# One slope behind the loop and a share of the scaled one-hot copies on GpSimd, in the logit stage of a graph network kernel

## The chip, the cores and the metric

The kernel runs on one core of a Trainium2 chip. The metric is the device time of one execution in microseconds; the median of several runs is quoted, and one execution is profiled. Engines are called as the profile calls them: PE (TensorE), DVE (VectorE), ACT (ScalarE), POOL (GpSimd), SP (SyncE, which only issues DMAs here).

## The reference

Four graph layers run one after the other over 3125 nodes and 100000 edges sorted by destination; each is followed by a layer norm over `x + layer(x)`. The change lies in the second layer, an attention layer. What is computed there:

```
h  = x @ Wn.T + bn;   e = edge_attr @ We.T + be
a  = leaky_relu(sum((h[src] + e) * attn, -1), 0.01)      # one logit per edge
m  = segment_max(a, dst)                                 # largest logit of each destination
a  = exp(a - m[dst]);  a = a / segment_sum(a, dst)[dst]
out = relu(segment_sum(h[src] * a, dst))
```

The leaky ReLU with slope 0.01 is max(z, 0.01 z), and it rises with z, so the largest logit of a node is the leaky ReLU of its largest z.

## The kernel before

Nodes are cut into 25 blocks of 125; edges are sorted into chunks of 128 (one edge for each partition), and a "group" is ten chunks. Each edge has one-hot rows, stored in DRAM as bf16, that say which node of a block it points to. The stage in question is `phase_logits` (tiles whose names begin with `lm_` in the trace). It computes z for each edge, the logit, and `negated`, which holds minus the largest logit of each destination node. The logits are kept in the second word of `words` (`srt_words` in the trace; a column of every second float, 4992 columns) and go on to the attention phase that follows.

The main loop runs over 119 groups, in 25 blocks of destination nodes. For each group g:

- SP loads the group's source plane (`load_planes`, line 1163) and its two halves of one-hot rows (`load_hot`, line 1171) into rings of four buffers. Before it refills a ring slot it waits for the engine that read it: `expanded` for the planes, `lifted` for the one-hot rows.
- DVE expands the plane into a one-hot of source nodes (`expand`, line 1217); PE looks the node values up in ten small products (`look`, line 1356), in three bf16 parts.
- DVE adds the three parts (line 1223, `total`), adds the edge part kept in `logit` (line 1225), applies the slope (line 1229) and subtracts a floor, a lower bound of all logits, so that what is stored is not negative (line 1230, `logits`). This raises `ready`.
- ACT multiplies each of the ten chunks' one-hot rows with the edge's value (line 1322) into one of two `raised` buffers and raises `lifted`. It waits for `ready`, for the one-hot rows, and for `grouped`, which says that DVE has read the buffer two groups back.
- DVE merges the raised buffer into `top8`: a copy for the first group of a block (line 1237), a maximum for the others (line 1239, `greater`). At the end of a block it reduces `top8` over the ten chunks (line 1288).

The order on DVE is written out by hand in `step(g)`: `expand(g + 3)`, then total and logits of group g + 2, then `greater(g)`. So PE has from the end of one `expand` to the `total` of the next step for its look, and ACT works one to two groups ahead of `greater`. Behind the loop PE transposes the 25 blocks of maxima (line 1371), DVE takes the maximum over the partitions (line 1300), builds diagonal matrices (line 1303), and PE spreads these over all partitions (line 1376). GpSimd does a single memset in this stage (line 1328).

A `Chain` object raises a semaphore with an instruction and makes its engine wait for it, so that the next instruction may read the result.

Of the kernel before, what the change touches and what calls it, by code (L numbers as in the profile page):

```python
# [8 lines left out]
ALU = mybir.AluOpType  # L9
ACT = mybir.ActivationFunctionType  # L10
AX = mybir.AxisListType
ds = bass.ds
# [5 lines left out]
P = 125  # L18
NB = N // P
EC = E // P  # L20
L = 128
# [3 lines left out]
RING = 4  # L25
# [142 lines left out]
def turns_of(eng, k):  # L168

    return eng.value_load(k["group_start"][0:1, 30:31], min_val=1, max_val=NT)  # L170
# [961 lines left out]
def phase_logits(nc, k, logit, negated, scratch):  # L1132
    ctx = ExitStack()
    with ctx:
# [14 lines left out]
        hot_landed, hot_arrived = [s.sem(f"hot_landed{r}") for r in range(RING)], s.sem("hot_arrived")  # L1149
        arrived, flipped, copied, written = (s.sem(n) for n in ("arrived", "flipped", "copied", "written"))  # L1150
        bounded, gathered, floored, cleared = (s.sem(n) for n in ("bounded", "gathered", "floored", "cleared"))
        split, chain_sem = s.sem("split"), s.sem("chain")
        expanded, looked, summed, ready, lifted, grouped = (
            s.sem(n) for n in ("expanded", "looked", "summed", "ready", "lifted", "grouped"))
        joined, passed, turned, ended = (s.sem(n) for n in ("joined", "passed", "turned", "ended"))
        PZ = 4

        with nc.Block() as block:

            @block.sync  # L1160
            def _(sp):
                def load_planes(g, j):
                    sp.dma_start(planes[:, j % RING, :], k["src_rows"][ds(G * g, G), :].rearrange("c l -> (c l)").partition_broadcast(L)
                                 ).then_inc(landed[j % RING], 16)

                unit_at = Offsets(sp, s, "unit", k["unit_at"], NUA - 1)

                def load_hot(g, j):
                    unit_at.load(g)
                    for t, unit in enumerate(unit_at.pair()):  # L1170
                        sp.dma_start(hot[:, j % RING, HALF * S * t:HALF * S * t + HALF * S],
                                     k["hot"][DST][ds(unit, 1), :, :].rearrange("o p n -> (o p) n")).then_inc(hot_landed[j % RING], 16)

                for b in range(BLOCKS):
                    if b % BANKS == BANKS - 1 or b == BLOCKS - 1:
                        b0 = b // BANKS * BANKS
                        sp.wait_ge(copied, b + 1)
                        sp.dma_start(k["src_rows"][b0 * L:(b + 1) * L, :].rearrange("(b c) l -> c b l", c=L), rows[:, b0:b + 1, :]
                                     ).then_inc(written, 16)
                load_hot(0, 0)  # L1180
                sp.wait_ge(written, 16 * WRITES)
                for j in range(3):
                    load_planes(j, j)
                sp.wait_ge(landed[0], 16)
                sp.sem_inc(arrived, 1)
                def turn(i, last):
                    for j in range(RING):
                        g = RING * i + j
                        sp.wait_ge(expanded, g + 2)
                        sp.sem_inc(passed, 1)  # L1190
                        load_planes(g + 3, j + 3)
                        sp.wait_ge(landed[(j + 1) % RING], 16 * (i + (j + 1) // RING) + 16)
                        sp.sem_inc(arrived, 1)
                        sp.wait_ge(lifted, g + 1)
                        sp.sem_inc(passed, 1)
                        if not last or j < 3:
                            load_hot(g + 1, j + 1)
                        sp.wait_ge(hot_landed[j], 32 * i + 32)
                        sp.sem_inc(hot_arrived, 1)

                turns = full_turns_of(sp, k)
                with sp.Fori(0, turns) as i:
                    turn(i, False)
                turns = full_turns_of(sp, k)
                turn(turns, True)
                for j in range(1, 3):
                    sp.wait_ge(landed[j], 16 * turns + 32)
                    sp.sem_inc(arrived, 1)

            @block.vector  # L1210
            def _(dve):
# [9 lines left out]
                def total(chain, g):  # L1221
                    dve.wait_ge(looked, g + 3)
                    chain(v.tensor_reduce(z[:, :], ps[:, ds((g % PZ) * 512, 3 * G)].rearrange("p (c t) -> p c t", t=3), AX.X, ALU.add))
                    dve.sem_inc(summed, 1)  # L1224
                    chain(v.tensor_tensor(z[:, :], z[:, :], logit[:, ds(G * g, G)], ALU.add))

                def logits(chain, g):
                    at = logit[:, ds(G * g, G)]
                    chain(v.scalar_tensor_tensor(z[:, :], z[:, :], 0.01, z[:, :], ALU.mult, ALU.max))
                    v.tensor_scalar(at, z[:, :], floor[:, :], None, ALU.subtract).then_inc(ready, 1)  # L1230

                def greater(g, first):
                    lift = raised[:, ds(g % 2, 1), :].rearrange("p a n -> p (a n)")
                    dve.wait_ge(lifted, g + 4)
                    dve.wait_ge(grouped, g + 2)
                    if first:
                        ins = v.tensor_copy(top8[:, :], lift)  # L1237
                    else:
                        ins = v.tensor_tensor(top8[:, :], top8[:, :], lift, ALU.max)
                    ins.then_inc(grouped, 1)  # L1240
# [10 lines left out]
                v.tensor_copy(v3[:, :, 2], rest[:, :]).then_inc(split, 1)  # L1251
                dve.wait_ge(gathered, 1)
                chain(v.tensor_reduce(low[:, 0:2], bank(7)[0:1, 0:2 * L].rearrange("p (t l) -> p t l", t=2), AX.X, ALU.min))
                chain(v.tensor_tensor(low[:, 2:3], low[:, 0:1], low[:, 1:2], ALU.add))
                v.scalar_tensor_tensor(low[:, 3:4], low[:, 2:3], 0.01, low[:, 2:3], ALU.mult, ALU.max).then_inc(bounded, 1)
                dve.wait_ge(gathered, 2)
                chain(v.tensor_copy(floor[:, :], bank(7)[:, 256:257]))
                for sem, head in ((summed, PZ), (grouped, 2), (joined, 1), (expanded, 2)):
# [2 lines left out]
                expand(1)  # L1261
                total(chain, 0)
                expand(2)
                logits(chain, 0)
                dve.wait_ge(ready, 1)
                total(chain, 1)
                logits(chain, 1)
                n = chain.n
                dve.sem_inc(passed, 1)

                def step(g, first):
                    chain = Chain(dve, chain_sem, n + 3 * g)
                    expand(g + 3)
                    dve.wait_ge(ready, g + 2)
                    total(chain, g + 2)
                    logits(chain, g + 2)
                    greater(g, first)
                    assert chain.n == 3

                with dve.Fori(0, NB) as d:  # L1280
                    g0, g1 = group_range(dve, k, d)
# [9 lines left out]
                with dve.Fori(g1, turns_of(dve, k) * RING) as g:  # L1291
                    dve.wait_ge(looked, g + 4)
                    dve.sem_inc(expanded, 1)
                    dve.wait_ge(looked, g + 5)
                    dve.sem_inc(summed, 1)
                    dve.sem_inc(ready, 1)
                    dve.wait_ge(lifted, g + 4)
                    dve.sem_inc(grouped, 1)
                dve.wait_ge(turned, 1)
                v.tensor_reduce(greatest[:, :], ps[0:P, 0:NB * L].rearrange("p (b l) -> p b l", l=L), AX.X, ALU.max).then_inc(ended, 1)  # L1300
                dve.wait_ge(ended, 1)
                for b in range(NB):
                    ins = v.tensor_scalar(diag[:, b, :], k["ident"][0:P, 0:P], greatest[:, b:b + 1], -1.0, ALU.mult, ALU.mult)
                ins.then_inc(ended, 1)
# [4 lines left out]
            @block.scalar  # L1309
            def _(act):  # L1310
                for b in range(BLOCKS):
                    act.wait_ge(flipped, b + 1)
                    nc.scalar.copy(rows[:, b, :], bank(b % BANKS)[:, 0:L]).then_inc(copied, 1)
                act.sem_inc(lifted, 3)
                with act.Fori(0, turns_of(act, k)) as i:
                    for j in range(RING):
                        g = RING * i + j
                        act.wait_ge(ready, g + 1)
                        act.wait_ge(hot_arrived, g + 1)
                        act.wait_ge(grouped, g + 1)  # L1320
                        for c in range(G):
                            ins = nc.scalar.activation(raised[:, j % 2, c * P:(c + 1) * P], hot[:, j, c * S:c * S + P], ACT.Copy,  # L1322
                                                       scale=logit[:, ds(G * g + c, 1)])
                        ins.then_inc(lifted, 1)

            @block.gpsimd
            def _(pool):
                nc.gpsimd.memset(ones[:, :], 1.0).then_inc(cleared, 1)

            @block.tensor  # L1330
            def _(pe):
# [8 lines left out]
                ins.then_inc(gathered, 1)  # L1340
                pe.wait_ge(cleared, 1)
                pe.wait_ge(bounded, 2)
                t_.matmul(bank(7)[:, 256:257], ones[0:1, :], low[:, 3:4], start=True, stop=True).then_inc(gathered, 1)
                pe.wait_ge(split, 1)
                pe.wait_ge(copied, BLOCKS)
                at = Offsets(pe, s, "at", k["block_at"], HALF * (HALF - 1))
# [1482 lines left out]
```

## Time and profile before

| what | value |
|---|---|
| median of 3 runs | 4012.24 us (3999.35 to 4015.62) |
| the profiled execution | 4001.7 us, of which the span is 4000.0 us |
| main loop of the logit stage | 1990 to 2416 us of the span, 426 us |
| its tail, to the copy of `negated` | 2416 to 2445 us |
| DVE, ACT, PE and POOL busy in the loop | 358.7, 356.2, 168.4 and 0 us |

Times in the profile are microseconds from the start of the span, single durations nanoseconds where marked. A row of the timeline gives start, length, engine, line, operation, output and inputs, the count of instructions merged into it, and in brackets how long the engine sat idle before it and what released it. A row of the groups gives the busy time of all instructions of one line, the mean length of one, and the idle time before them with its releasers. ACT's instructions overlap in part, so forty of 385 ns fill 11.84 us.

### The profile page before, as it was taken

How to read it: one execution, taken by the hardware profiler on the slowest of the kernel's cores; microseconds unless marked ns; L12 is line 12 of the kernel's file. 1: busy time of each engine (PE TensorE's matmuls, PEld its weight loads, DVE VectorE, ACT ScalarE, POOL GpSimd, SP SyncE). 2: the span in 40 equal slices, each digit the busy share in tenths (PEclk: the TensorE clock that was granted, in tenths of full speed). 3: DMA queues.
4: the chain of work that ended last, by engine and by line, in shares of the span. 5: the costliest groups of instructions: out<-in, count | busy, mean ns of one | idle time of the engine just before them, and what ended most of it. 6: DMA issues, size and time to landing. Idle time of an engine off the chain costs nothing. (4 is left out here: it accounts for less than half of the span.)

```text
span 4000.0 us, 83948 instructions
## 1 busy us (share of the span) xinstructions
PE 3158.0 (79%) x17737; PEld 2344.7 (59%) x17738; DVE 2479.1 (62%) x6639; ACT 1821.9 (46%) x6302; POOL 1235.7 (31%) x993
## 2 busy tenths in 40 slices
PE   5666667988887777989743335889999899999978
PEld 4444445888876756767632224778888444444455
DVE  7999998978875563234488886777766500001754
ACT  1888883344445542011298875777776000000111
POOL 1688888888888800111000000000000000002512
PEclk9999999999998888999855557999999999999989
DMA  2444445677878874767565553544332543541067
GB/s 96 125 121 121 123 121 116 183 215 237 239 239 273 274 275 143 230 194 207 163 213 184 183 168 108 151 130 119 113 98 79 188 138 109 192 154 55 0 219 254
DMA packets 438541, 654.87 MB, mean 164 GB/s; under 512 B 102707, under 2 KB 293812, under 8 KB 438314
## 3 DMA queue, kind: packets, MB, share of 16 engines
q1 hardware_dynamic: 350648, 516.48, 41.7%
q10 hardware_dynamic: 56434, 125.33, 8.7%
q0 software_dynamic: 31360, 11.85, 3.3%
q8 instruction: 49, 0.80, 0.1%
q14 instruction: 50, 0.41, 0.0%
HBM read 436.96 MB, written 215.57 MB: 163 GB/s over the span
## 5 line engine op out<-in xcount | busy, mean ns | idle before, releaser
L1069 POOL DMA_INDIRECT slots<-all_B,put_index x800 | 1044.9, 1306 | 343.2 <-issue 341.1
L2338 PE MATMUL gio_po<-gio_T,all_A 125*128 125x500 f32 (+1 forms) x1400 | 529.8, 540 | 6.1 <-DMA gio_T<-pair 6.1
L2338 PEld LDWEIGHTS gio_po<-gio_T,all_A 125*128 125x128 f32 x1400 | 249.4, 190 | 283.2 <-issue 276.4
L1322 ACT ACTIVATE lm_raised<-lm_hot,srt_words 128x125 f32<-128x125 bf16 x1200 | 356.2, 385 | 81.0 <-DVE lm_top L1237 63.8
L1356 PE MATMUL lm_ps<-lm_v,lm_node 125*128 x1220 | 170.5, 184 | 264.4 <-DVEq L1224 94.5
L1040 PE MATMUL put_ps<-put_right_in,put_left_in 128*128 128x125 f32 x2210 | 320.0, 295 | 66.3 <-ACT put_left_in L897 65.8
L2085 PE MATMUL att_ps<-att_right,att_left 128*125 128x125 f32 x2380 | 313.5, 285 | 70.5 <-ACT att_right L2106 67.3
L1635 PE MATMUL c_po<-c_halves,c_T 125*125 125x512 f32 x1250 | 330.0, 413 | 22.8 <-DMA c_T<-counts 13.1
L2085 PEld LDWEIGHTS att_ps<-att_right,att_left 128*125 128x125 f32 x2380 | 283.9, 189 | 96.1 <-issue 85.8
L1040 PEld LDWEIGHTS put_ps<-put_right_in,put_left_in 128*128 128x128 f32 x2210 | 282.1, 203 | 90.3 <-ACT put_left_in L897 76.2
L2159 DVE SCALAR_TENSOR_TENSOR att_power<-soft_negated,srt_words,att_far 128x125 f32 (+1 forms) x1190 | 320.4, 345 | 3.7 <-ACT att_right L2106 3.3
L1356 PEld LDWEIGHTS lm_ps<-lm_v,lm_node 125*128 125x128 bf16 x1220 | 127.0, 104 | 307.9 <-issue 283.8
L1044 PE MATMUL put_ps<-put_right_out,put_left_out 128*128 128x125 f32 x2210 | 303.8, 287 | 0.0
L2647 DVE SCALAR_TENSOR_TENSOR upd_pre<-sum_u,sum_sums,upd_bias 125x512 f32<-125x512 f32 x25 | 27.7, 1109 | 423.6 <-POOL upd_bias L2561 422.8
L1635 PEld LDWEIGHTS c_po<-c_halves,c_T 125*125 125x125 f32 x1250 | 232.5, 190 | 95.6 <-DVE c_halves L1727 21.7
L897 ACT CAST put_left_in<-put_hot 128x640 f32 (+1 forms) x221 | 161.5, 731 | 275.8 <-DVE put_hot L811 159.9
L1044 PEld LDWEIGHTS put_ps<-put_right_out,put_left_out 128*128 128x128 f32 x2210 | 284.1, 204 | 0.8
L2057 PE MATMUL att_ps<-all_A,all_B 125*125 125x257 f32 x1250 | 277.5, 381 | 0.6 <-ACT att_sums L2110 0.6
L816 DVE TENSOR_TENSOR put_right_in<-put_hot,put_words_in 128x625 f32<-128x625 bf16 x224 | 181.9, 812 | 150.2 <-PE put_ps L1040 144.9
L2106 ACT ACTIVATE att_right<-att_power 128x250 f32<-128x250 f32 x595 | 242.9, 408 | 55.2 <-DVE att_power L2159 54.0
L2103 ACT CAST att_left<-att_ring 128x250 f32 x595 | 229.2, 385 | 74.8 <-SPq L231 39.1
L2057 PEld LDWEIGHTS att_ps<-all_A,all_B 125*125 125x125 f32 x1250 | 231.5, 187 | 38.9 <-issue 0.9
(440 smaller groups left out, 5308.0 us busy)
## 6 DMA issues: line engine op xcount, KB each, us to landing
c_T<-counts SPq DMA_DIRECT2D x255, 312.5 KB, 3.4
pair<-put_T ACTq DMA_DIRECT2D x125, 625.0 KB
att_ring<-hot SPq DMA_DIRECT2D x480, 160.0 KB
gio_T<-pair SPq DMA_DIRECT2D x60, 1250.0 KB, 5.9
hot<-put_hot SPq DMA_DIRECT2D x448, 160.0 KB
all_A<-in_edge_attr_dram SPq DMA_DIRECT2D x100, 448.0 KB
lm_planes<-src_rows SPq DMA_DIRECT2D x123, 320.0 KB, 3.6
counts<-put_T ACTq DMA_DIRECT2D x125, 312.5 KB
```

What stands on the lines that cost most here:

```text
L1040: ins = t_.matmul(tile(1, c), left_in[:, c, :], right_in[:, c, :], start=False, stop=False, skip_group_check=True)
L1044: ins = t_.matmul(tile(2, c), left_out[:, c, :], right_out[:, c, :], start=False, stop=False, skip_group_check=True)
L1069: nc.gpsimd.indirect_dma_start(slots, bass.IndirectOffsetOnAxis(index[:, C * g + j:C * g + j + 1], 0), stage[:, C * g + j, :], None).then_ ...
L1322: ins = nc.scalar.activation(raised[:, j % 2, c * P:(c + 1) * P], hot[:, j, c * S:c * S + P], ACT.Copy, scale=logit[:, ds(G * g + c, 1)])
L1356: ins = t_.matmul(bank(j % PZ)[0:L, 3 * c:3 * c + 3], node[0:P, j % 2, L * c:L * c + L], v3[:, ds(units[c // HALF], HALF), :][:, c % HALF, :],
L1635: return t_.matmul(po[0:P, d % BANKS, 0:2 * width], T[0:P, n % LOOK, t * P:(t + 1) * P].bitcast(fp32r), halves[:, PB * q + t, :], start=(q ...
L2057: ins = t_.matmul(product(0), T[h][:, q, :], H[:, q, 0:width], start=(q == 0), stop=(q == NB - 1))
L2085: ins = t_.matmul(tiles_of(ps)[:, ds(units[(W * f + c) // HALF], HALF), :][:, (W * f + c) % HALF, 0:P], left[:, f, c, :], right[:, f, c, : ...
L2103: nc.scalar.copy(left[:, f, :, :], ring.slot(r, lf, W * f, W * f + W)).then_inc(left_ready.sem(f), 1)
L2106: nc.scalar.activation(right[:, f, :, :], power[:, f, :, :], ACT.Exp).then_inc(right_ready.sem(f), 1)
L2159: ins = v.scalar_tensor_tensor(power[:, f, c, :], negated[:, ds(d, 1), :].rearrange("p a n -> p (a n)"), logit[:, ds(G * g + q, 1)], far[: ...
L2338: ins = t_.matmul(po[:, i % 2, h, 0:w], A[:, b, 128 * h:128 * h + 128], tiles, start=(b == 0), stop=(b == NB - 1))
```

## The change

1. `total` no longer ends with the sum of node part and edge part, and `logits` is gone. One instruction, `(z - floor) + at`, writes the value without the slope and raises `ready`; two of DVE's small operations of each group go. The floor is made without the slope too (one operation less ahead of the loop).
2. Behind the loop a new `slope` adds the floor back and applies the slope, in two instructions over all 4992 columns of `logit`; after the maxima over the partitions it does the same for the 125 by 25 maxima. It stands ahead of DVE's wait for PE's transposes and waits for ACT's last group.
3. ACT makes eight of a group's ten scaled copies. GpSimd makes the other two in one `tensor_tensor` product over 2 x 125 elements: the one-hot rows (bf16) times the two values (f32, each spread over 125 elements), into the same `raised` buffer (f32). It waits for the same three semaphores as ACT and raises `hoisted`. SP's refill of the one-hot ring and DVE's `greater` wait for `hoisted` beside `lifted`.

```diff
-                    chain(v.tensor_tensor(z[:, :], z[:, :], logit[:, ds(G * g, G)], ALU.add))
-
-                def logits(chain, g):
                     at = logit[:, ds(G * g, G)]
-                    chain(v.scalar_tensor_tensor(z[:, :], z[:, :], 0.01, z[:, :], ALU.mult, ALU.max))
-                    v.tensor_scalar(at, z[:, :], floor[:, :], None, ALU.subtract).then_inc(ready, 1)
+                    v.scalar_tensor_tensor(at, z[:, :], floor[:, :], at, ALU.subtract, ALU.add).then_inc(ready, 1)
+
+                def slope(t, parts):
+                    chain(v.tensor_scalar(t, t, floor[0:parts, :], None, ALU.add))
+                    chain(v.scalar_tensor_tensor(t, t, 0.01, t, ALU.mult, ALU.max))
...
                     dve.wait_ge(lifted, g + 4)
+                    dve.wait_ge(hoisted, g + 4)
...
+                turns = turns_of(dve, k)
+                dve.wait_ge(lifted, turns * RING + 3)
+                chain = Chain(dve, sloped)
+                slope(logit, L)
                 dve.wait_ge(turned, 1)
                 v.tensor_reduce(greatest[:, :], ...).then_inc(ended, 1)
                 dve.wait_ge(ended, 1)
+                slope(greatest[:, :], P)
...
-                        for c in range(G):
+                        for c in range(LIFTS):
...
+                pool.sem_inc(hoisted, 3)
+                with pool.Fori(0, turns_of(pool, k)) as i:
+                    for j in range(RING):
+                        g = RING * i + j
+                        pool.wait_ge(ready, g + 1)
+                        pool.wait_ge(hot_arrived, g + 1)
+                        pool.wait_ge(grouped, g + 1)
+                        by_chunk = (lambda t, w: t.rearrange("p (c n) -> p c n", n=w)[:, :, 0:P])
+                        nc.gpsimd.tensor_tensor(by_chunk(raised[:, j % 2, LIFTS * P:], P), by_chunk(hot[:, j, LIFTS * S:], S),
+                                                logit[:, ds(G * g + LIFTS, G - LIFTS)].unsqueeze(2).to_broadcast([L, G - LIFTS, P]), ALU.mult
+                                                ).then_inc(hoisted, 1)
```

## Rows read from the trace of the kernel before

**Rows 1.** Busy times of the loop: PE, PEld, DVE, ACT, POOL, clock, DMA.

```profile
1990.00:2416.00 426.00, 168.37 (x1205) 125.39 (x1205) 358.68 (x746) 356.23 (x1200) 0.00 (x0) 0.50 0.59 183
```

**Rows 2.** Groups of instructions in the loop: busy us, mean ns, idle before.

```profile
L1322 ACT ACTIVATE lm_raised<-lm_hot,srt_words 128x125 f32<-128x125 bf16 x1200 | 356.2, 385 | 81.0 <-DVE lm_top L1237 63.8 <-DVE srt_words L1230 12.2 <-DVE lm_top L1239 3.6
L1239 DVE TENSOR_TENSOR lm_top<-lm_top,lm_raised 128x1250 f32<-128x1250 f32 x94 | 137.4, 1461 | 0.4
L1217 DVE TENSOR_SCALAR lm_node<-lm_planes,all_iop x119 | 65.3, 549 | 18.1 <-DVE soft_negated L1288 14.6 <-PE lm_ps L1356 2.1 <-SPq L1193 0.7
L1288 DVE TENSOR_REDUCE soft_negated<-lm_top 128x1250 f32 x25 | 62.2, 2486 | 3.7
L1225 DVE TENSOR_TENSOR lm_z<-lm_z,srt_words 128x10 f32<-128x10 f32 x120 | 20.4, 170 | 32.9 <-DVE lm_z L1223 32.8
L1237 DVE COPY lm_top<-lm_raised 128x1250 f32 x25 | 20.3, 812 | 0.1
```

**Rows 3.** Timeline of one block of five groups.

```profile
2103.63 0.55 DVE L1217 TENSOR_SCALAR lm_node<-lm_planes,all_iop  x1 [0.64 <-DVE soft_negated L1288]
...
2105.93 0.55 DVE L1217 TENSOR_SCALAR lm_node<-lm_planes,all_iop  x1
...
2106.66 0.19 DVE L1223 TENSOR_REDUCE lm_z<-lm_ps 128x10 f32 x1 [0.18 <-PE lm_ps L1356]
...
2109.15 0.55 DVE L1217 TENSOR_SCALAR lm_node<-lm_planes,all_iop  x1
2109.46 11.84 ACT L1322 ACTIVATE lm_raised<-lm_hot,srt_words 128x125 f32<-128x125 bf16 x40 [0.21 <-DVE lm_top L1239]
...
2112.09 0.55 DVE L1217 TENSOR_SCALAR lm_node<-lm_planes,all_iop  x1
2112.55 0.18 DVE L1223 TENSOR_REDUCE lm_z<-lm_ps 128x10 f32 x1
...
2113.01 0.17 DVE L1225 TENSOR_TENSOR lm_z<-lm_z,srt_words 128x10 f32<-128x10 f32 x1 [0.27 <-DVE lm_z L1223]
...
2113.43 0.23 DVE L1230 TENSOR_SCALAR srt_words<-lm_z,lm_floor 128x10 f32 x1
2113.66 1.46 DVE L1239 TENSOR_TENSOR lm_top<-lm_top,lm_raised 128x1250 f32<-128x1250 f32 x1
...
2115.04 0.55 DVE L1217 TENSOR_SCALAR lm_node<-lm_planes,all_iop  x1
...
2118.22 2.48 DVE L1288 TENSOR_REDUCE soft_negated<-lm_top 128x1250 f32 x1
...
2121.34 0.55 DVE L1217 TENSOR_SCALAR lm_node<-lm_planes,all_iop  x1 [0.64 <-DVE soft_negated L1288]
```

**Rows 4.** Timeline of SP's queue: plane loads of two turns, first block.

```profile
2013.48 0.33 SPq L1163 DMA_DIRECT2D lm_planes<-src_rows  x1
...
2015.96 0.33 SPq L1163 DMA_DIRECT2D lm_planes<-src_rows  x1
```

**Rows 5.** Timeline of other phases where GpSimd computes beside DVE.

```profile
3115.95 0.72 POOL L2253 TENSOR_TENSOR all_total<-all_total,all_X 125x256 f32<-125x256 f32 x1 [10.93 <-DVEq L2245]
...
3683.72 0.74 DVE L2647 SCALAR_TENSOR_TENSOR upd_pre<-sum_u,sum_sums,upd_bias 125x512 f32<-125x512 f32 x1
...
3689.28 1.66 POOL L2559 TENSOR_SCALAR upd_part<-sum_u,sum_sums 125x512 f32<-125x512 f32 x1 [0.79 <-DVE upd_pre L2650]
...
3691.02 1.36 POOL L2561 TENSOR_TENSOR upd_bias<-upd_part,sum_base 125x512 f32<-125x512 f32 x1
...
3691.75 1.18 DVE L2647 SCALAR_TENSOR_TENSOR upd_pre<-sum_u,sum_sums,upd_bias 125x512 f32<-125x512 f32 x1
```

**Rows 6.** Timeline behind the loop, and the reduction over the logit column.

```profile
2418.43 5.70 PE L1371 MATMUL lm_ps<-all_ident,soft_negated 128*125 128x128 f32 x25 [3.64 <-DVE soft_negated L1288]
2424.17 3.49 DVE L1300 TENSOR_REDUCE lm_greatest<-lm_ps 125x25 f32<-125x3200 f32 x1 [5.79 <-PE lm_ps L1371]
...
1970.90 5.35 DVE L1245 TENSOR_REDUCE lm_least<-srt_words 128x1 f32<-128x4992 f32 x1
```

More of the change, by code:

```diff
@@ L1151, in phase_logits @@
         bounded, gathered, floored, cleared = (s.sem(n) for n in ("bounded", "gathered", "floored", "cleared"))
-        split, chain_sem = s.sem("split"), s.sem("chain")
-        expanded, looked, summed, ready, lifted, grouped = (
-            s.sem(n) for n in ("expanded", "looked", "summed", "ready", "lifted", "grouped"))
+        split, chain_sem, sloped = s.sem("split"), s.sem("chain"), s.sem("sloped")
+        expanded, looked, summed, ready, lifted, hoisted, grouped = (
+            s.sem(n) for n in ("expanded", "looked", "summed", "ready", "lifted", "hoisted", "grouped"))
+        LIFTS = 8
         joined, passed, turned, ended = (s.sem(n) for n in ("joined", "passed", "turned", "ended"))
@@ L1194, in turn @@
                         sp.wait_ge(lifted, g + 1)
+                        sp.wait_ge(hoisted, g + 1)
                         sp.sem_inc(passed, 1)
@@ L1253, in _ @@
                 chain(v.tensor_reduce(low[:, 0:2], bank(7)[0:1, 0:2 * L].rearrange("p (t l) -> p t l", t=2), AX.X, ALU.min))
-                chain(v.tensor_tensor(low[:, 2:3], low[:, 0:1], low[:, 1:2], ALU.add))
-                v.scalar_tensor_tensor(low[:, 3:4], low[:, 2:3], 0.01, low[:, 2:3], ALU.mult, ALU.max).then_inc(bounded, 1)
+                v.tensor_tensor(low[:, 2:3], low[:, 0:1], low[:, 1:2], ALU.add).then_inc(bounded, 1)
                 dve.wait_ge(gathered, 2)
@@ L1263, in _ @@
                 expand(2)
-                logits(chain, 0)
                 dve.wait_ge(ready, 1)
                 total(chain, 1)
-                logits(chain, 1)
                 n = chain.n
@@ L1271, in step @@
                 def step(g, first):
-                    chain = Chain(dve, chain_sem, n + 3 * g)
+                    chain = Chain(dve, chain_sem, n + g)
                     expand(g + 3)
@@ L1275, in step @@
                     total(chain, g + 2)
-                    logits(chain, g + 2)
                     greater(g, first)
-                    assert chain.n == 3
+                    assert chain.n == 1
                 with dve.Fori(0, NB) as d:
@@ L1297, in _ @@
                     dve.wait_ge(lifted, g + 4)
+                    dve.wait_ge(hoisted, g + 4)
                     dve.sem_inc(grouped, 1)
+                turns = turns_of(dve, k)
+                dve.wait_ge(lifted, turns * RING + 3)
+                chain = Chain(dve, sloped)
+                slope(logit, L)
                 dve.wait_ge(turned, 1)
@@ L1342, in _ @@
                 pe.wait_ge(bounded, 2)
-                t_.matmul(bank(7)[:, 256:257], ones[0:1, :], low[:, 3:4], start=True, stop=True).then_inc(gathered, 1)
+                t_.matmul(bank(7)[:, 256:257], ones[0:1, :], low[:, 2:3], start=True, stop=True).then_inc(gathered, 1)
                 pe.wait_ge(split, 1)
```

## The prediction

> **What bounds the kernel now.** I read the loop's stretch first (busy times by engine), then its groups with their idle times, then the timeline of one block. In the loop, 426.0 us, DVE is busy 358.68 us and ACT 356.23 us; PE is busy 168.37 us, POOL not at all [rows 1]. Two engines with equal loads don't say which sets the pace; the idle columns do. ACT's 81.0 us of idle time are nearly all ended by DVE: 63.8 us by the copy L1237, the first merge of a block, 12.2 us by the first logits, 3.6 us by L1239 [rows 2]. DVE in turn waits for nobody who matters: before L1239 it sat idle 0.4 us in 94 merges and before L1237 0.1 us, so ACT is never late; PE and SP together end 2.8 us ahead of L1217. What DVE loses is its own: 32.8 us ahead of L1225 (the result of L1223 has to land first) and 14.6 us at the turn of a block [rows 2]. So DVE's order of work is the path. In the timeline the reader is to see the period of a step: the expansions start at 2109.15, 2112.09 and 2115.04, 2.945 us apart, and L1223, L1225, L1230 and L1239 follow with no gap but L1225's 0.27. The first step of a block has the shorter copy and takes 2105.93 - 2103.63 = 2.30 us; a whole block of five takes 14.59 us to the start of its reduction (2118.22) and 3.12 us from there to the next block (2121.34) [rows 3]. Copies (25), merges (94) and reductions (25) in [rows 2] give 119 steps in 25 blocks; the reductions of the timeline split them into one block of 18, two of 8, nine of 5, one of 4 and twelve of 3.
>
> **DVE's two operations.** From the start of L1225 to that of L1230 is 2113.43 - 2113.01 = 0.42 us; then L1230 takes 0.23 until L1239 starts at 2113.66 [rows 3]. The new instruction has the same column of floors as an operand as L1230, so I give it L1230's 0.23 us, and 0.42 us go from each step. The 0.27 us behind L1223 stay, since the new instruction reads z too. Its other results are awaited where they were: `ready` an expansion later, `lifted` and `hoisted` while the instruction runs. The second of the waits is taken to cost nothing because the sequencer does it under these 0.23 us; without that cover I would add some hundredths of a microsecond to each step. A step with a merge would become 2.945 - 0.42 = 2.53 us.
>
> **What PE gives back.** A look starts when its expansion is done and the next step's L1223 waits for it. The wait is visible once: L1223 at 2106.66 had waited 0.18 us for PE, 3.03 us after the expansion of 2103.63 [rows 3]. So L1223 can't come earlier than 3.03 us after the expansion of the step before. In the second step of each block this holds already; the 0.42 us that the first step gains are lost there again. The gain is thus 0.42 us for 119 - 25 = 94 steps, 39.5 us. Further on in a block the rule spans two steps: 3.03 us plus the 2.48 - 0.42 = 2.06 us from L1223 to the next expansion (2112.55 to 2115.04 before) is 5.09, or 2.55 us a step in place of 2.53. Over 69 steps that is 1.5 us. Left: 38 us.
>
> **ACT, SP and the memory.** Forty activations took 11.84 us [rows 3], 0.296 us each, so eight take 2.37 us a group in place of 2.96. That is under DVE's 2.53; ACT gains slack and the end gains nothing from it alone. Without it DVE's shorter step would have run into ACT's 2.96 us, so this part is what makes the first part worth anything. SP's plane loads follow each other 2.48 us apart where its queue doesn't wait [rows 4], with one more semaphore wait to come: below 2.55, but barely. Blocks of up to 8 are covered by the 3.12 us of the block turn; the first block, of 18 steps, starts without that lead and I charge 1 us. DMA's share of 0.59 [rows 1] would rise by a tenth, and the clock of TensorE, granted at 0.50 (the 1.2 GHz level) in this stretch [rows 1], is taken to stay.
>
> **GpSimd's product.** Nothing in the loop shows one. The nearest row is L2253, 256 f32 elements in 0.72 us; L2561 takes 1.36 us for 512 [rows 5], so 250 elements are about 0.7 us. It starts when `grouped` rises, some 0.2 us behind the end E of a merge (ACT had 0.21 us of idle time there [rows 3]), and is needed two steps later: as work it is hidden. What it can cost is DVE's time. [Rows 5] show it: L2647 takes 0.74 us where no POOL operation starts beside it and 1.18 us when it starts inside L2561, at 3691.75; it was held for 0.44 us, to 3692.19, 0.19 us ahead of L2561's recorded end (3692.38). In the new loop the instruction at risk is the new sum, which like L2647 reads two tiles of SBUF. It would start 0.92 us behind an expansion (2113.01 - 2112.09), which is E + 0.84 since the expansion starts 0.08 us before E (2115.04 against 2113.66 + 1.46). The product runs from E + 0.2 to E + 0.92 and lets go at E + 0.73: no delay. That is the low end; a gain below nothing is excluded, since the product takes over no DVE work. If it is itself held by the expansion, to E + 0.47, it lets go at E + 1.00, a delay of 0.16 us; if it then also holds to its recorded end, E + 1.19, the delay is 0.35 us. No row shows whether an expansion holds a product. I take 0.10 us, because part of a product's start can pass while it waits. It applies in the steps whose sum follows a merge within the same block by less than 1.5 us: all but the first two of a block (there the second waits for PE anyway, and behind the last merge the reduction lies), 119 - 50 = 69. Cost 7 us.
>
> The Trainium skill, SBUF — State Buffer, section Who interferes with whom, goes further: a DVE instruction with two SBUF inputs and a GpSimd one that reads SBUF exclude each other for the whole instruction, and a two-port DVE operation locks GpSimd out as well. The rows agree that DVE is held, and disagree by 0.19 us on how long. By that rule the delay is the 0.35 us above; it is the first rival below.
>
> **The tail.** Behind the last reduction DVE waited for PE's transposes, from 2418.43 to 2424.17 [rows 6]. The slope now fills this wait: two operations over 4992 columns. The reduction over the same column took 5.35 us [rows 6]; the second, with two inputs, gets this. The first has one input: 5.35 us at worst, at best the rate of the copy L1237 (1250 in 0.812 us [rows 2]), some 2.8 us for 4992, by an estimate that keeps its 0.16 us of overhead. Together 8.2 to 10.7 us, of which 5.7 lie beside the transposes: 2.5 to 5.0 us late. The slope of the maxima adds two instructions of about 0.2 us, on the path. I take 4.2 us. The floor's shorter chain ahead of the loop saves one small operation, 0.2 us, which I leave out: the first expansion waits for loads.
>
> **Sum.** 39.5 - 1.5 - 1 - 7 - 4.2 = 25.8 us saved, rounded to 26. Against the profiled execution (4001.7 us, span 4000.0) that is 3976 us. That execution lies 10.5 us under the median of the runs, which the forecast is for: 4012.24 - 26 = 3986 us. With the bounds (delay 0 to 0.25, tail 2.9 to 5.4) the saving is 14 to 34 us: 3978 to 3998.
>
> **Rivals.**
> - *The product holds the sum to its end* (0.35 us or a little more, up to 0.45). 69 steps cost 24 to 31 us, and of 37 us 2 to 9 are left behind the tail: about 4006 us, no change. For it: the 0.44 us of L2647. Against it: L2647 went on before the product ended. Chance 0.2.
> - *The product is long, and slower is the result.* Its input is bf16 and one operand is spread, and no row shows either on POOL. L2559 took 1.66 us [rows 5]. A product of that length, let go 0.19 us before its end and held by the expansion as above, ends at E + 0.47 + 1.66 - 0.19 = E + 1.94: 1.1 us of delay in 69 steps is 76 us against 37, so 43 us slower with the tail, 4055 us; at half that excess, 1.2 us of length, it is even. The point is a delay of (37 - 4.2) / 69 = 0.48 us. For it: unknown types. Against it: L2253 and L2561. Chance 0.12.
> - *SP sets the step.* If its turn is 2.75 us with the extra wait, long blocks gain half: 16 steps of the first and 12 of the blocks of 8, 0.2 us each, some 6 us. With the tail, 25 us of gain become 20: near the border. Chance 0.08, shared between faster and same.
>
> **How the numbers follow.** The forecast has 0.6. About 0.5%, 20 us, is what a measurement of this kernel tells from no change; the runs before spread over 16 us. The forecast's own range reaches below that bound at its far end, so of its 0.6 I put 0.51 to faster, 0.08 to same, 0.01 to slower; with SP's 0.04 and the rivals this makes faster 0.55, same 0.32, slower 0.13. The range runs from 3970, the best bound less the spread of the median, to 4014, which takes in the first rival and leaves out the long product.
>
> **What would show it.** Right: expansions 2.55 to 2.7 us apart within long blocks; one instruction of 0.23 us in place of L1225, L1229 and L1230; L1223 of second steps waiting some 0.6 us for PE; ACT idle between most groups; L1300 2.5 to 5 us later behind the last reduction than now. Wrong: a sum that takes 0.4 us or more beside a product, products over 1 us long, or expansions that wait for SP. A step under 2.5 us would say that PE's 3.03 us were read wrongly.

## The result and the profile after

The changed kernel takes 3979.3 us (median of 4 runs, 3976.4 to 3985.8), the kernel before 4007.7 us in 4 runs. The ratio is 0.9932, with a 95% interval of 0.9906 to 0.9958: 17 to 38 us less, by the medians 28 us. The forecast was 26 us less, 3986 us against 4012.2.

The profiled execution of the changed kernel has a span of 3984.1 us, 15.9 less than before; the stage itself explains more than that. From its first instruction on DVE to the end of the copy of `negated` it takes 449.1 us in place of 473.9, which is 24.8 us less; the other phases, in which nothing changed, happened to take 9 us longer in this execution. So the stage is compared here, not the span. Its parts:

| part of the stage | before | after | difference |
|---|---|---|---|
| up to the first step of the loop | 23.2 us | 23.1 us | -0.1 |
| loop: expansion of its first step to the end of the last reduction | 424.6 us | 395.3 us | -29.3 |
| tail: to the end of the copy of `negated` | 26.1 us | 30.7 us | +4.6 |

A block of five of the changed kernel in the timeline (the expansion is now L1219, the reduction of z L1225, the new sum L1228, copy and merge L1240 and L1242, GpSimd's product L1342):

```profile
2097.26 0.55 DVE L1219 TENSOR_SCALAR lm_node<-lm_planes,all_iop  x1 [0.64 <-DVE soft_negated L1287]
...
2099.22 0.55 DVE L1219 TENSOR_SCALAR lm_node<-lm_planes,all_iop  x1
...
2100.29 0.19 DVE L1225 TENSOR_REDUCE lm_z<-lm_ps 128x10 f32 x1 [0.53 <-PE lm_ps L1372]
...
2102.43 0.55 DVE L1219 TENSOR_SCALAR lm_node<-lm_planes,all_iop  x1
...
2102.80 0.63 POOL L1342 TENSOR_TENSOR lm_raised<-lm_hot,srt_words 128x250 f32<-128x250 bf16 x1 [2.58 <-DVE lm_top L1242]
...
2103.35 0.23 DVE L1228 SCALAR_TENSOR_TENSOR srt_words<-lm_z,lm_floor,srt_words 128x10 f32 x1 [0.28 <-DVE lm_z L1225]
2103.64 1.46 DVE L1242 TENSOR_TENSOR lm_top<-lm_top,lm_raised 128x1250 f32<-128x1250 f32 x1
...
2105.02 0.55 DVE L1219 TENSOR_SCALAR lm_node<-lm_planes,all_iop  x1
...
2107.61 0.55 DVE L1219 TENSOR_SCALAR lm_node<-lm_planes,all_iop  x1
...
2110.43 2.50 DVE L1287 TENSOR_REDUCE soft_negated<-lm_top 128x1250 f32 x1
```

Against [rows 3]: the first step takes 1.96 us in place of 2.30; the second still takes 3.21, and its reduction now waits 0.53 us for PE in place of 0.18; the steps after it take 2.59 in place of 2.945. The product runs for 0.63 us beside the expansion and the reduction and is over at 2103.43, 0.08 us behind the start of the sum, which takes its 0.23 us undisturbed. Behind the sum there is something new: the merge starts 0.29 us after the sum's start; before, it started 0.23 us after that of L1230.

The groups of the stage:

```profile
L1327 ACT ACTIVATE lm_raised<-lm_hot,srt_words 128x125 f32<-128x125 bf16 x960 | 291.0, 386 | 115.8 <-DVE lm_top L1240 70.7 <-DVE lm_top L1242 34.6 <-DVE srt_words L1228 10.5
...
L1242 DVE TENSOR_TENSOR lm_top<-lm_top,lm_raised 128x1250 f32<-128x1250 f32 x94 | 137.3, 1461 | 5.9
...
L1342 POOL TENSOR_TENSOR lm_raised<-lm_hot,srt_words 128x250 f32<-128x250 bf16 x120 | 75.4, 628 | 338.1 <-DVE lm_top L1242 199.1 <-DVE lm_top L1240 116.3 <-DVE srt_words L1228 18.9
...
L1228 DVE SCALAR_TENSOR_TENSOR srt_words<-lm_z,lm_floor,srt_words 128x10 f32 x119 | 27.3, 229 | 33.4 <-DVE lm_z L1225 33.4
L1225 DVE TENSOR_REDUCE lm_z<-lm_ps 128x10 f32 x119 | 21.8, 183 | 12.8 <-PE lm_ps L1372 12.8
```

ACT and POOL wait for DVE almost alone, as ACT did in [rows 2]; the merges now have 5.9 us of idle time ahead of them (0.4 before), and the reductions of z wait 12.8 us for PE (2.5 before).

The tail, against [rows 6]:

```profile
2387.97 2.46 DVE L1287 TENSOR_REDUCE soft_negated<-lm_top 128x1250 f32 x1
...
2391.65 2.82 DVE L1231 TENSOR_SCALAR srt_words<-srt_words,lm_floor 128x4992 f32<-128x4992 f32 x1 [1.22 <-issue]
2394.50 5.36 DVE L1232 SCALAR_TENSOR_TENSOR srt_words<-srt_words 128x4992 f32<-128x4992 f32 x1
2399.89 3.49 DVE L1304 TENSOR_REDUCE lm_greatest<-lm_ps 125x25 f32<-125x3200 f32 x1
2403.42 0.24 DVE L1231 TENSOR_SCALAR lm_greatest<-lm_greatest,lm_floor 125x25 f32<-125x25 f32 x1
2403.70 0.18 DVE L1232 SCALAR_TENSOR_TENSOR lm_greatest<-lm_greatest 125x25 f32<-125x25 f32 x1
```

The maximum over the partitions starts 9.46 us behind the end of the last reduction (2390.43); before it was 5.80. With the 0.5 us for the maxima that is 4.2 us on DVE's path; the other 0.4 us of the table's 4.6 lie in PE's spreading, 8.62 us here and 8.23 before, which took 7.2 to 8.8 us in the kernels below.

### The profile page after: what moved, and what is told of

The parts are those of the page before. It is cut to its first block and busy times, and to the rows that moved or that the text cites. A ratio compares the mean times of both kernels' runs of the same rounds, so it can differ in the third digit from the quotient of the medians.

```text
span 3984.1 us, 83543 instructions
## 1 busy us (share of the span) xinstructions
PE 3166.4 (79%) x17737; PEld 2352.9 (59%) x17738; DVE 2444.4 (61%) x6400; ACT 1756.8 (44%) x6062; POOL 1307.6 (33%) x1113
## 5 line engine op out<-in xcount | busy, mean ns | idle before, releaser
L1327 ACT ACTIVATE lm_raised<-lm_hot,srt_words 128x125 f32<-128x125 bf16 x960 | 291.0, 386 | 115.8 <-DVE lm_top L1240 70.7
L2122 ACT ACTIVATE att_right<-att_power 128x250 f32<-128x250 f32 x595 | 242.9, 408 | 52.2 <-DVE att_power L2175 51.3
```

The costliest lines, as they stand in the source:

```text
L2122: nc.scalar.activation(right[:, f, :, :], power[:, f, :, :], ACT.Exp).then_inc(right_ready.sem(f), 1)
```

## The experiments

In all kernels the loop is the stretch of the table above, and the ratio is to the kernel before on the same chip.

| kernel | loop | block of 5 | first block, of 18 | ratio to before (95%) |
|---|---|---|---|---|
| before | 424.6 us | 14.5 to 14.6 us | 53.6 us | 1 |
| after | 395.3 | 13.1 to 13.2 | 50.8 | 0.9932 (0.9906 to 0.9958) |
| ten copies on ACT | 397.5 | 13.1 to 13.2 | 52.2 | 0.9929 (0.9914 to 0.9945) |
| GpSimd's share alone | 426.5 | 14.6 to 14.8 | 53.3 | 1.0001 (0.9990 to 1.0011) |
| four copies on GpSimd | 403.3 | 13.5 to 13.6 | 51.5 | 0.9951 (0.9934 to 0.9967) |
| DVE's waits early | 391.8 | 12.8 to 13.0 | 52.8 | 0.9922 (0.9906 to 0.9938) |
| slope late | 396.3 | 13.1 to 13.2 | 52.1 | 0.9934 (0.9916 to 0.9952) |
| PE's load late | 382.9 | 12.6 | 53.0 | 0.9902 (0.9885 to 0.9918) |
| slope and load late | 382.9 | 12.5 | 53.5 | 0.9907 (0.9890 to 0.9924) |
| the same, ten copies on ACT | 385.5 | 12.8 | 52.1 | 0.9906 (0.9890 to 0.9922) |
| all three moves | 378.9 | 12.3 | 53.7 | 0.9886 (0.9865 to 0.9907) |

**One part undone: ten copies on ACT.**

```diff
-        LIFTS = 8
+        LIFTS = G
...
-                    dve.wait_ge(hoisted, g + 4)
...
-                        nc.gpsimd.tensor_tensor(...).then_inc(hoisted, 1)
```

> The changed kernel with one part undone: ACT makes all ten copies again, GpSimd none, no wait for hoisted; DVE's shorter step and the slope behind the loop stay. The prediction said that without GpSimd's share DVE's shorter step would run into ACT's ten copies (2.96 us a group). If ACT sets the pace in that way the steps in long blocks go from 2.59 back to 2.96 us, the loop takes 415 to 425 us as before, and with 4 us for the slope the kernel takes as long as the kernel before or 4 us more. Rival: ACT catches up during the reduction at each block's end (it stood idle 2.65 us a block before), so only the long blocks pay; then ten copies cost some 7 us against the changed kernel, the loop takes about 402 us and the kernel is still about 20 us (0.5%) faster than before.

The kernel is as fast as the changed one: 0.9929 and 0.9932. The loop is 2.2 us longer. A long block shows where ten copies do cost something:

```profile
2057.29 0.55 DVE L1218 TENSOR_SCALAR lm_node<-lm_planes,all_iop  x1
2057.60 20.38 ACT L1324 ACTIVATE lm_raised<-lm_hot,srt_words 128x125 f32<-128x125 bf16 x70 [0.24 <-DVE lm_top L1240]
...
2059.86 0.55 DVE L1218 TENSOR_SCALAR lm_node<-lm_planes,all_iop  x1
...
2062.42 0.55 DVE L1218 TENSOR_SCALAR lm_node<-lm_planes,all_iop  x1
...
2066.59 1.46 DVE L1240 TENSOR_TENSOR lm_top<-lm_top,lm_raised 128x1250 f32<-128x1250 f32 x1 [0.36 <-ACT lm_raised L1324]
```

The steps are 2.56 to 2.57 us while ACT lives on its lead, seventy activations run without a pause, and not before the sixth step of this block of eight does a merge wait, 0.36 us; so do the two after it. Blocks of three to five end before that, and during their reduction ACT catches up. The rival holds: GpSimd's share is worth a few microseconds in the long blocks at most, less than the runs can tell. Without the wait for `hoisted` each step is 0.03 us shorter, which hides a part of what ten copies cost.

**The other part alone.** The kernel before with `LIFTS = 8`, GpSimd's product and the waits for `hoisted`; DVE's operations as before.

> The kernel before with the other part alone: ACT makes eight copies and GpSimd two, DVE's four small operations a step are as before. If DVE alone sets the pace, and the product ends before DVE's next two-input sum, nothing changes but ACT's idle time (+70 us): loop 424 to 432 us, kernel within 0.2% of the kernel before. If the product holds DVE's operations, the sum L1225 would be longer than 0.17 us and steps longer than 2.95 us: 69 steps by 0.16 to 0.35 us, 11 to 24 us slower.

The ratio is 1.0001. So DVE alone sets the pace, and with the run before, the whole gain of the change comes from its two operations. The steps are a little longer than before:

```profile
2084.25 0.55 DVE L1219 TENSOR_SCALAR lm_node<-lm_planes,all_iop  x1
...
2084.62 0.63 POOL L1341 TENSOR_TENSOR lm_raised<-lm_hot,srt_words 128x250 f32<-128x250 bf16 x1 [2.34 <-DVE lm_top L1242]
...
2085.17 0.17 DVE L1227 TENSOR_TENSOR lm_z<-lm_z,srt_words 128x10 f32<-128x10 f32 x1 [0.27 <-DVE lm_z L1225]
...
2087.22 0.55 DVE L1219 TENSOR_SCALAR lm_node<-lm_planes,all_iop  x1
```

2.97 us, 0.03 more than in [rows 3], with every operation as long as it was; the sum keeps its 0.17 us beside the product. The only thing that DVE got here is the wait for `hoisted`. The run before says the same from the other side: without that wait its steps are 2.56 to 2.57 us where the changed kernel has 2.59. The rows of DVE's instruction queue (DVEq, its sequencer) agree. The wait instruction ahead of a merge, in the kernel before, in this one and in the one with ten copies (least, median and greatest length in ns):

```profile
L1235 DVEq EVENT_SEMAPHORE  x119: 21/21/21, 1995.2 to 2414.1; - x119
L1238 DVEq EVENT_SEMAPHORE  x119: 49/50/50, 1993.8 to 2414.6; - x119
L1236 DVEq EVENT_SEMAPHORE  x119: 21/21/21, 1997.8 to 2390.0; - x119
```

**A longer product: four copies on GpSimd.** `LIFTS = 6`, nothing else.

> The changed kernel with GpSimd making four of ten copies in its product and ACT six. The product of two took 0.60 to 0.63 us, so four should take 1.1 to 1.25 us and end 1.4 to 1.55 us behind the merge before it, where the sum wants to start 0.84 us behind it. If a product that reads SBUF holds a DVE operation with two SBUF inputs, the sum waits 0.4 to 0.65 us in 69 steps: loop 22 to 45 us longer than the changed kernel's 395 us, kernel as slow as the kernel before or slower, steps in long blocks 3.0 to 3.2 us. If the two don't hold each other, the steps stay at 2.59 us and the kernel at the changed kernel's time, since ACT and GpSimd both end long before the merge needs them.

```profile
2087.03 0.54 DVE L1219 TENSOR_SCALAR lm_node<-lm_planes,all_iop  x1
...
2087.39 1.05 POOL L1342 TENSOR_TENSOR lm_raised<-lm_hot,srt_words 128x500 f32<-128x500 bf16 x1 [1.69 <-DVE lm_top L1242]
...
2087.94 0.53 DVE L1228 SCALAR_TENSOR_TENSOR srt_words<-lm_z,lm_floor,srt_words 128x10 f32 x1 [0.28 <-DVE lm_z L1225]
...
2088.39 1.45 DVE L1242 TENSOR_TENSOR lm_top<-lm_top,lm_raised 128x1250 f32<-128x1250 f32 x1
2089.76 0.54 DVE L1219 TENSOR_SCALAR lm_node<-lm_planes,all_iop  x1
```

The product does hold the sum: 0.53 us in place of 0.23. It was held for 0.30 us, to 2088.24, and the product ends at 2088.44, 0.20 us later; the 0.19 us of [rows 5] come back. It is held in 66 of the 94 steps with a merge. But the step is only 0.15 us longer (2.73 to 2.75), the loop 8 us and not 22 or more. The merge starts 0.45 us after the sum's start, inside its recorded length: the 0.06 us that the changed kernel loses between sum and merge are hidden under the longer sum. The theory stands; the hold is shorter than the 0.4 to 0.65 us that I expected, and half of it is given back.

**DVE's waits early.**

```diff
                     dve.wait_ge(ready, g + 2)
+                    dve.wait_ge(lifted, g + 4)
+                    dve.wait_ge(hoisted, g + 4)
+                    dve.wait_ge(grouped, g + 2)
                     total(chain, g + 2)
```

(and out of `greater`).

> The changed kernel with DVE's three waits (lifted, hoisted, grouped) of a step moved from between the new sum and the merge to ahead of the reduction that begins the sum. In the changed kernel the merge starts 0.06 us later behind the sum's end than it did before; the step is 2.59 us where 2.53 was forecast. If it is the sequencer working through the waits, the gap goes to 0.01 and steps to 2.53 us: 119 steps by 0.06, 7 us less (0.18%). If it is the register work for the merge's address, nothing changes.

```profile
2078.34 0.23 DVE L1228 SCALAR_TENSOR_TENSOR srt_words<-lm_z,lm_floor,srt_words 128x10 f32 x1 [0.28 <-DVE lm_z L1225]
2078.52 1.46 DVE L1239 TENSOR_TENSOR lm_top<-lm_top,lm_raised 128x1250 f32<-128x1250 f32 x1
```

The merge starts 0.18 us after the sum's start in place of 0.29, so the time between them was the waits. The step falls by less, to alternating 2.49 and 2.61 us: every other reduction comes some 0.12 us late. The profile names GpSimd's product as its releaser, but the semaphores in the trace say that it is ACT: in all 20 late cases the wait ended 0.03 us after ACT had raised `lifted`, and GpSimd had been done for 1.76 us. ACT's groups then follow without a pause, here ahead of a late reduction at 2080.48:

```profile
2077.72 4.92 ACT L1327 ACTIVATE lm_raised<-lm_hot,srt_words 128x125 f32<-128x125 bf16 x16 [0.75 <-DVE lm_top L1239]
2077.78 0.63 POOL L1342 TENSOR_TENSOR lm_raised<-lm_hot,srt_words 128x250 f32<-128x250 bf16 x1 [2.55 <-DVE lm_top L1239]
```

Two groups of eight take 4.92 us, 2.46 each: with the waits early, ACT's eight copies nearly fill DVE's step of 2.49. The loop is 3.5 us shorter, and the ratio can't be told from that of the changed kernel.

**Slope late.**

```diff
-                slope(logit, L)
                 dve.wait_ge(turned, 1)
...
                 ins.then_inc(ended, 1)
+                slope(logit, L)
                 dve.wait_ge(turned, 2)
```

> The changed kernel with the slope over the 4992 columns moved behind the 25 diagonal products, where DVE waits 8.8 us for PE's spreading. The two operations take 8.2 us, so they fit under this wait. In the changed kernel the maximum over the partitions came 3.7 us later behind the last reduction than before, and 0.5 us more go to the slope of the maxima, which stays. If the tail's price is where the slope stands, the tail gets 3.5 to 4 us shorter and the loop stays at 395 us: 0.1% less than the changed kernel. If the copy of the result has to wait longer for the slope than for PE, less.

```profile
2398.79 4.94 DVE L1307 TENSOR_SCALAR all_B<-all_ident,lm_greatest 125x125 f32<-125x125 f32 x25
2403.65 2.81 DVE L1231 TENSOR_SCALAR srt_words<-srt_words,lm_floor 128x4992 f32<-128x4992 f32 x1
...
2403.88 7.29 PE L1392 MATMUL lm_ps<-all_B,lm_ones 125*128 125x125 f32 x50 [9.22 <-DVE all_B L1307]
2406.50 5.36 DVE L1232 SCALAR_TENSOR_TENSOR srt_words<-srt_words 128x4992 f32<-128x4992 f32 x1
2411.89 3.42 DVE L1311 COPY soft_negated<-lm_ps 128x3125 f32<-128x3125 f32 x1
```

The slope lies beside PE's spreading and the copy starts 24.3 us behind the start of the last reduction, in place of 29.7 (25.1 before the change). PE's spreading was also 1.3 us shorter in this execution, but the copy now waits for the slope, which ends at 2411.86, and not for PE, which is done at 2411.17. So 4 to 5 of the 5.4 us are the move's, as expected or a little more. In the kernel's time it is too little to be seen.

**PE's load late.**

```diff
                     for c in range(G):
-                        if c == G // 2:
-                            at.load(g + 1)
                         ins = t_.matmul(...)
                     ins.then_inc(looked, 1)
+                    at.load(g + 1)
```

> The changed kernel with PE's register load of the next group's positions moved from the middle of a look (where PE stands 0.65 us between the fifth and the sixth product) to behind its last product. The second step of a block takes 3.1 to 3.25 us because its reduction waits for PE, 3.03 us behind the expansion before. If that wait is the look's own length, the look gets 0.65 us shorter and the second step goes to 2.6 us: 25 steps by 0.5 to 0.6 us, 12 to 15 us less than the changed kernel (0.3 to 0.4%). Rival: the load only moves ahead of the next look, and where two looks follow each other, as in a second step, the reduction is as late as before; then nothing or a few us.

```profile
2092.59 0.55 DVE L1219 TENSOR_SCALAR lm_node<-lm_planes,all_iop  x1 [0.64 <-DVE soft_negated L1287]
...
2093.37 1.33 PE L1370 MATMUL lm_ps<-lm_v,lm_node 125*128 x10 [4.56 <-DVEq L1226]
...
2094.54 0.55 DVE L1219 TENSOR_SCALAR lm_node<-lm_planes,all_iop  x1
...
2095.00 0.18 DVE L1225 TENSOR_REDUCE lm_z<-lm_ps 128x10 f32 x1
...
2097.14 0.55 DVE L1219 TENSOR_SCALAR lm_node<-lm_planes,all_iop  x1
```

A look is now 1.33 us in one piece, the second reduction comes 2.41 us behind the expansion before it and waits for nobody, and the second step takes 2.60 us. The loop is 12.4 us shorter and the ratio 0.9902. The gain that PE took back is there to be had.

**The moves together, with and without GpSimd.** `e8_both` has the slope and the load late, `e9_no_share` has both and ten copies on ACT, `e10_three_moves` has both, the early waits, and GpSimd's share.

> The changed kernel with both moves of the two runs beside it: the slope under PE's spreading and PE's load behind the look. If the two add up, 16 to 19 us less than the changed kernel, about 3961 us where the kernel before takes 4008.

> The same two moves, but with all ten copies on ACT and nothing on GpSimd. With ten copies a group ACT had no price at steps of 2.57 us in short blocks because it catches up while DVE reduces. With the second step shorter ACT has less time per block: five groups take 14.8 us of ACT's time, and a block of five would take about 15.6 us. Reckoned by the rows, ACT then holds DVE in steps of blocks of five and more, and this kernel is 7 to 9 us slower than the one with GpSimd's share. If ACT still catches up, the two are equal and the share is worth nothing here either.

> The changed kernel with all three moves: DVE's waits ahead of the reduction, the slope under PE's spreading, PE's load behind the look. Now that the look is 0.65 us shorter, PE no longer holds the second step, and the moved waits should give their 0.06 us in every step outside the first block: 101 steps, 6 us less than with the two moves (loop 377 us against 382.9), kernel about 0.15% below it. Rival: the first block, which SP's queue sets, takes 52 to 54 us whatever DVE's step is, and the moved waits make the reduction wait for GpSimd's product or ACT's copies in second steps, so that nothing is left.

The two moves together have the loop of the one and the tail of the other; the ratio, 0.9907, is that of PE's load alone within its interval. Against the changed kernel that is some 10 us by the ratios, where 16 to 19 were expected: the slope's move doesn't show in the kernel's time here either. Without GpSimd the loop is 2.6 us longer, not 7 to 9, and the ratio the same: even with the shorter steps ACT holds DVE only in the last steps of blocks of five and more. All three moves give 0.9886, 3958.5 us against 4003.0; the loop's 378.9 us are 4 less than with two, where 6 were expected: in 38 steps the reduction comes some 0.12 us late, again 0.03 us behind ACT's `lifted`. It is the fastest kernel here.

## Why the prediction was right, point by point

The total, 26 us against 28 by the medians and 24.8 in the profiled stage, was right, but that it came so near is luck. With the measured terms in the same order, 39.5 - 1.5 - 1 - 7 - 4.2 becomes 33.4 - 0 - 3.2 - 0 - 4.6 = 25.6: DVE's gain was 6 us too large, the first block cost 2 us more than charged, and the 7 us for GpSimd's product and the 1.5 us for PE, which didn't come in that way, paid for both.

- **DVE as the path.** Right. GpSimd's share alone moves nothing (1.0001), DVE's two operations alone give all (0.9929).
- **0.42 us a step, with the waits hidden.** Too large. The step lost 0.355 us. The sum itself has the forecast 0.23 us; the cover was the mistake. The sequencer has to work through three waits and an address before the merge, and the new sum's 0.23 us are not long enough for it: the move of all three waits brings the merge 0.11 us nearer, to 0.18 us. So the 0.23 us between L1230 and the merge in [rows 3], which I read as the length of L1230, left no room for a further wait either: GpSimd's share alone made every step 0.03 us longer. That wait is half of the 0.06 us. The other half is there without it, 2.56 to 2.57 us with ten copies on ACT where 2.53 were forecast, and what it comes from stays open. I had named this price, "some hundredths of a microsecond", and set it to nothing. Over 94 steps it takes 6 us: 33.4 us where 39.5 were forecast.
- **PE gives nothing in the second step.** Right, and shown by moving PE's load: 3.12 to 3.25 us before and after, 2.60 us with the look 0.65 us shorter. The further 1.5 us, for later steps at 2.53 against 2.55, didn't arise, since the steps are 2.59.
- **GpSimd's product delays the sum by 0.10 us.** Wrong: not at all. The product takes 0.60 us alone and 0.63 beside an expansion, less than the 0.72 of [rows 5], so the expansion hardly holds it, and by the 0.20 us of the longer product it lets go at 0.63 - 0.20 = 0.43 us behind its start, 0.1 us ahead of the sum (2102.80 and 2103.35 give 0.55). The low end of the bounds was the right one; the mechanism is real, and four copies instead of two bring it into the loop. With two it shows in the first block alone, and on the expansion, not on the sum: three expansions that came late met a product and were held, by 0.8 us together.
- **ACT's relief makes the rest worth anything.** Wrong. I compared 2.96 us a group with DVE's step and left out the time in which ACT catches up, 3.12 us at each block's end, though the 63.8 us of idle time in [rows 2] had shown it. The share could have been left out; whether it could with DVE's waits early too was not tried.
- **SP in the first block, 1 us.** Too small. The first block gained 2.8 us where 17 steps by 0.355 make 6.0. In all kernels here it takes 50.8 to 53.7 us; before, DVE's steps of 2.945 us fill it, and the faster kernels wait in it. SP's own waits in this block of the changed kernel are one row (line, releaser, total, times, longest):

```profile
SPq L1201 <- DMA lm_hot<-hot: 2.5, 6, 0.7
```

  and in the later blocks, where SP waits for DVE and for ACT in turn:

```profile
SPq L1191 <- DVE lm_node L1219: 34.7, 22, 2.1
SPq L1197 <- ACT lm_raised L1327: 24.2, 36, 1.0
```

  So in the first block SP waits for 2.5 us out of 51 and works through its queue the rest; its plane loads of 1999.67 to 2045.28 follow each other 2.49 us apart at the least and 2.85 on average. That this queue sets the block is in the trace: six expansions make DVE wait, 2.5 us together, and each starts 0.36 to 0.37 us behind SP's signal that a plane is there. With the 0.8 us of the held expansions that is about the 3.2 us that are missing. A kernel with less work on SP was not tried.
- **The tail, 4.2 us.** Right: 3.7 and 0.5. The first operation had the copy's rate, the good end (2.82 us against a forecast of 2.8 to 5.35), and lost it again to 1.22 us in which DVE had nothing to do but to reach it in its program. The Trainium skill, VectorE: DVE Perf Modes, section Mode 2×_2P, gives a one-input f32 operation within SBUF two elements a cycle; the strided column in 2.82 us agrees, beside 5.36 us for the two-input operation over the same elements.
- **The rivals.** A product that holds the sum to its recorded end would have made it 0.08 us longer in the block shown; it takes 0.23 us with GpSimd's product and without, so this one didn't come. For any delay the product would have needed a start or an end more than 0.1 us later; the margin is thin, and the four copies show what lies behind it. The long product didn't come: with bf16 and a spread operand 250 elements took 0.60 to 0.63 us in nearly all steps, less than the 0.72 of L2253. Its border of 1.2 us was wrong by the prediction's own numbers, which give 1.04 us for a delay of 0.48; the four copies, 1.05 us long, cost 0.15 us a step and left the kernel faster than before. SP's rival came true in the first block alone.

## What to carry to other kernels

Before crediting an engine's relief, undo it alone: an engine with nearly the busy time of the bound, but waiting for it in a few places, has slack that its mean time per group hides. A wait that is already satisfied cost the sequencer some 0.03 us here, hidden only while a long enough operation runs in front of it; when small operations are merged, put the waits of the next large one further ahead. And a reduction that was late by 0.18 us becomes the place where the next gain is lost: shorten what it waits for in the same change. Where a wait stands on several semaphores, look up which of them rose last before believing the engine that a profile names.

## What the runs showed of the hardware

Which of two operations starts first decides who is held. In nearly all steps the expansion starts 0.34 to 0.38 us ahead of the product and neither is longer than alone by more than 0.03 us. In the first block it came late several times; in the first pair below it still starts first, by 0.08 us, in the second the product does:

```profile
2000.53 0.55 DVE L1219 TENSOR_SCALAR lm_node<-lm_planes,all_iop  x1 [0.21 <-issue]
2000.61 0.93 POOL L1342 TENSOR_TENSOR lm_raised<-lm_hot,srt_words 128x250 f32<-128x250 bf16 x1 [2.52 <-DVE lm_top L1242]
...
2008.73 0.60 POOL L1342 TENSOR_TENSOR lm_raised<-lm_hot,srt_words 128x250 f32<-128x250 bf16 x1 [1.96 <-DVE lm_top L1242]
2008.77 0.91 DVE L1219 TENSOR_SCALAR lm_node<-lm_planes,all_iop  x1 [0.33 <-PE lm_ps L1372]
```

In the first pair the product took 0.93 us in place of 0.60; in the second it kept its 0.60 us and the expansion took 0.91 in place of 0.55. The other such pairs of the block fit one reckoning: a product 0.17 us behind an expansion took 0.84 us, expansions 0.12 and 0.25 us behind a product took 0.83 and 0.70. In each the second operation is longer by what is missing to 0.40 or 0.41 us behind the start of the first. The Trainium skill, SBUF — State Buffer, section Who interferes with whom, has it so: issue order decides who blocks. What it says beyond, that the first one holds the ports for the whole instruction, does not fit the recorded ends: in [rows 5] and with four copies DVE went on 0.19 and 0.20 us ahead of the product's recorded end, the expansions here 0.20 us, and the products went on 0.14 us ahead of the expansion's. Whether the records run on behind the last access, no run here shows.

A product over 250 elements with bf16 input and a spread f32 operand took 0.60 us on GpSimd, over 500 elements 1.02 us: 1.7 ns for each further element. A held operation can also be cheap: while DVE's sum was held for 0.30 us its sequencer went on with the waits and the address of the merge, and half of the delay was given back.
